# A selective scan's sums over its states, made for two scan units at once instead of for each

## The reference

```
x = x + cross_attention(layernorm(x), ctx)   # 16 heads, quantised query and output projections
x = x + scan_block(layernorm(x))
x = x + mixture_of_experts(layernorm(x))     # 64 experts, top 8, capacity 512 rows
```

```
xp = x @ x_proj_w.T;  dt_low, b, c = split(xp)
dt = softplus(dt_low @ dt_proj_w.T + dt_proj_b);  a = -exp(A_log)
h[t] = exp(dt[t] * a) * h[t-1] + dt[t] * x[t] * b[t]      # for each channel and state
y[t] = sum over the 16 states of h[t] * c[t]
out  = y + x * D_param
```

## Time and profile before

| | |
|---|---|
| time, median of 3 runs | 2230.54 us (2229.82 to 2233.25) |
| the profiled execution's own time | 2231.84 us |
| its span | 2230.1 us |
| PE busy | 2087.4 us, 94% |
| PE weight loads busy | 1431.6 us, 64% |
| DVE busy | 1631.8 us, 73%, 3522 instructions |
| ACT busy | 1519.4 us, 68% |
| POOL busy | 597.7 us, 27% |
| mean granted TensorE clock | 0.972 of full speed |

### The profile page before, as it was taken

How to read it: one execution, slowest core, us unless ns; L and a number is a source line. 1 busy time by engine, 2 the same in 40 slices (tenths; PEclk the granted TensorE clock), 3 DMA queues, 4 the chain that set the end, 5 groups by cost and what they waited for, 6 DMA issues and landing times. The chain is left out here.

```text
span 2230.1 us, 54255 instructions
## 1 busy us (share of the span) xinstructions
PE 2087.4 (94%) x20746; PEld 1431.6 (64%) x20746; DVE 1631.8 (73%) x3522; ACT 1519.4 (68%) x3140; POOL 597.7 (27%) x604
## 2 busy tenths in 40 slices
PE   7999999999999999999999999999998559989965
PEld 4666666666666666666666666666665448868854
DVE  4447777878787878687878787777778747767746
ACT  2667776767686868676767777777768237757753
POOL 0001030303030312122121213030303127767770
PEclk9999999999999999999999999999999569999988
DMA  6475762213232222222222222221201147666748
GB/s 214 172 264 213 263 215 102 98 48 101 63 92 74 73 74 73 75 76 74 72 79 67 83 75 87 77 93 53 99 16 60 63 132 222 211 223 210 220 131 339
DMA packets 114271, 277.26 MB, mean 124 GB/s; under 512 B 19851, under 2 KB 70711, under 8 KB 107872
## 3 DMA queue, kind: packets, MB, share of 16 engines
q1 hardware_dynamic: 95584, 239.10, 32.7%
q0 software_dynamic: 18432, 34.69, 4.4%
HBM read 165.40 MB, written 108.27 MB: 123 GB/s over the span
## 5 line engine op out<-in xcount | busy, mean ns | idle before, releaser
L989 DVE TENSOR_REDUCE sb_negmax<-S 128x1 f32<-128x1604 f32 x256 | 467.7, 1827 | 145.6 <-PE S L622 139.7
L808 ACT ACTIVATE sb_probsT<-W 128x384 f32<-128x384 f32 (+1 forms) x1024 | 476.1, 516 | 90.7 <-PE W L632 86.5
L816 ACT ACTIVATE sb_probs<-S,sb_negmax 128x1604 f32<-128x1604 f32 x256 | 409.3, 1599 | 113.1 <-DVE sb_negmax L989 113.0
L632 PEld LDWEIGHTS W<-sb_ident,sb_probs 128*128 128x128 f32 (+1 forms) x3328 | 365.4, 139 | 185.8 <-ACT sb_K L800 133.3
L632 PE MATMUL W<-sb_ident,sb_probs 128*128 128x128 f32 (+1 forms) x3328 | 464.4, 278 | 6.5 <-ACT sb_probsT L808 2.5
L607 PE MATMUL W<-sb_wkv_in,sb_ctx 128*128 128x256 f32 (+1 forms) x1664 | 406.1, 386 | 14.3 <-ACT sb_probsT L808 12.4
L597 PE MATMUL W<-sb_ctx,sb_wkv_in 128*32 128x401 f32 x4096 | 399.0, 503 | 1.5 <-DMA sb_ctx<-ctxT 1.5
L800 ACT ACTIVATE sb_K<-W,sb_pair_cols 128x401 f32<-128x401 f32 x256 | 152.7, 596 | 279.9 <-PE W L597 279.8
L607 PEld LDWEIGHTS W<-sb_wkv_in,sb_ctx 128*128 128x128 f32 (+1 forms) x1664 | 293.4, 187 | 74.2 <-ACT sb_probsT L808 38.2
L1369 POOL DMA_INDIRECT y_scratch<-sb_ys,sb_places x256 | 254.0, 992 | 109.1 <-issue 74.4
L622 PE MATMUL S<-sb_K,sb_Q 32*128 32x400 f32 (+1 forms) x2048 | 244.3, 546 | 7.3 <-ACT sb_probs L816 6.1
(11 more groups left out here) (197 smaller groups left out, 2813.4 us busy)
## 6 DMA issues: line engine op xcount, KB each, us to landing
sb_ctx<-ctxT SPq DMA_DIRECT2D x32, 1604.0 KB, 7.6
xe_scratch<-sb_none SPq DMA_DIRECT2D x32, 1088.0 KB, 12.2
sb_xg<-xe_scratch SPq DMA_DIRECT2D x64, 544.0 KB, 4.1
sb_BC<-bc_scratch SPq DMA_DIRECT2D x32, 1024.0 KB, 6.2
sb_Q<-sb_q_own SPq DMA_DIRECT2D x128, 128.0 KB, 4.1
y_scratch<-sb_none SPq DMA_DIRECT2D x16, 1024.0 KB, 12.0
sb_rows<-y_scratch SPq DMA_DIRECT2D x16, 1024.0 KB, 8.1
sb_wgu<-wgu SPq DMA_DIRECT2D x64, 192.0 KB
```

The lines of the kernel that those rows point to most:

```text
L632: ins = pe.transpose(W[0:keys_in(t), at * P:(at + 1) * P], probs[n % 2][:, t * P:t * P + keys_in(t)], ident[:])
L808: act.activation(probsT[k][n % (k + 1)][:, 0:wide], ring[bank_of("T", G, k)][:, 0:wide], ACT.Copy)\
L816: act.activation(probs[n % 2][:].rearrange("p (c k) -> p c k", c=QUADS), scores_of, ACT.Exp, bias=negmax[:, slot:slot + 1], accum_out=den[ ...
L989: dve.tensor_reduce(negmax[:, slot:slot + 1], scores_of, AX.XY, ALU.max, negate=True).then_inc(max_done, 1)
```

## The change

The sum over states is made once for two units. For the first unit of each two (q = 0 or 2 of a half) `sum_unit` returns at once. For the second the products of both units are added, 512 columns, and then halved twice and added onto y as before. `dve_y` rises by 2 at each of these sums, so that its values at the end of a pair stay the same, and POOL's wait for a quarter of `bx` ends with the sum of the two units. A pair has four chained operations fewer.

```diff
-B_LINKS, ROUTE_LINKS = 58, 9
+B_LINKS, ROUTE_LINKS = 54, 9
...
             def sum_unit(p, unit, link):

                 h, q = divmod(unit, NS // QS)
-                mine = bx[:, q * QS:(q + 1) * QS, :]
-                link(dve.tensor_tensor(mine[:, 0:2, :], mine[:, 0:2, :], mine[:, 2:4, :], ALU.add))
-                link(dve.tensor_tensor(mine[:, 0, :], mine[:, 0, :], mine[:, 1, :], ALU.add))
-                if q == 0:
-                    dve.scalar_tensor_tensor(y[:, h, :], ln2T[:, h, :], cols[:, DP, h:h + 1], mine[:, 0, :], ALU.mult, ALU.add)\
-                       .then_inc(dve_y, 1)
+                if q % 2 == 0:
+                    return
+                both = bx[:, (q - 1) * QS:q * QS, :]
+                link(dve.tensor_tensor(both, both, bx[:, q * QS:(q + 1) * QS, :], ALU.add))
+                link(dve.tensor_tensor(both[:, 0:2, :], both[:, 0:2, :], both[:, 2:4, :], ALU.add))
+                link(dve.tensor_tensor(both[:, 0, :], both[:, 0, :], both[:, 1, :], ALU.add))
+                if q == 1:
+                    dve.scalar_tensor_tensor(y[:, h, :], ln2T[:, h, :], cols[:, DP, h:h + 1], both[:, 0, :], ALU.mult, ALU.add)\
+                       .then_inc(dve_y, 2)
                 else:
-                    dve.wait_ge(dve_y, p * UNITS + unit)
-                    dve.tensor_tensor(y[:, h, :], y[:, h, :], mine[:, 0, :], ALU.add).then_inc(dve_y, 1)
+                    dve.wait_ge(dve_y, p * UNITS + unit - 1)
+                    dve.tensor_tensor(y[:, h, :], y[:, h, :], both[:, 0, :], ALU.add).then_inc(dve_y, 2)
```

## The result

| | before | after |
|---|---|---|
| time, median of 14 runs each | 2230.82 us | 2235.40 us |
| ratio, 95% interval | | 1.0019 (1.0011 to 1.0027) |
| profiled span | 2230.1 us | 2232.0 us |
| DVE busy | 1631.8 us | 1611.7 us |

The kernel is slower by 0.19%, 4.2 us by the ratio, although DVE does 20 us less. The time lies within the range and on the forecast's side; it is 2.4 us above the 2233.0 predicted, and just above the 2235.0 up to which I had called it no change.

What follows compares the result with a forecast made beforehand. PE's order of work was taken to set the pace in middle pairs, with DVE on the path only at the end. Costs of 0.7 + 1.8 = 2.5 us gave a predicted median of 2233.0 us, range 2228 to 2238.

Steps and rivals of the forecast that it cites:

- Hidden in the middle pairs: Pairs with scans beside PE's work: PE sets the pace, delays stay nearly hidden; 0.05 us a pair, 0.7 us total.
- The delays of the maxima behind units 1, 3, 5 and 7: Middle pairs, heavier steps: row maxima start 0.70, 0.53, 0.59 and 0.48 us late, nearly all covered by existing waits.
- The last stretch: Pair 14's scan inside pair 15: late maxima and unit 7's sum delay the output's turn 1.8 us; bounds 0 and 2.5.
- The 0.72 us of unit 7: Last stretch: unit 7's paired sum adds 0.72 us ahead of the output's turn, after its scan is 1.0 late.
- After the turn: Behind pair 14's output turn: one serial chain of DVE, PE and DMA to the experts, carrying the 1.8 us delay.
- Step 1 catching: Rival, middle pairs: keys' load follows the values' copy, 0.48 us arrives each pair, 6.7 us total, 2239.0; chance 0.11.
- The collision: Rival, steps of units 2 and 4: GpSimd's products hold up DVE's, 5.0 us if nothing hides it, 2237.3; chance 0.07.
- DVE's time counting: Rival, faster: all 1.5 us of DVE time saved per pair comes back, 23 us, giving 2208; chance 0.06.

Runs made afterwards that it cites:

- e6_no_sums: The changed kernel with its three additions over the states left out, one state of each two units reaching the output: 2228.84 us, ratio 0.9985 to before.
- e5_mended: The changed kernel with the output's semaphore rising by 1 per sum and the even units' products counted but not waited for at once: 2231.1 us (one run).
- e7_longer_unit7: The changed kernel with one more chained 512-column addition (692 ns) ahead of unit 7's output add: 2244.39 us (one run).
- e4_split: The changed kernel with both waits mended and halvings and output add moved to the next even unit's step, except units 6 and 7: 2234.21 us, ratio 1.0007.

## Why the prediction was right, and where it was not

**Hidden in the middle pairs.** Right: DVE's 1.3 us less a pair bring nothing, by the table and by e6_no_sums. The delays of the maxima behind units 1, 3, 5 and 7, which I had put at 0.70, 0.53, 0.59 and 0.48 us, are 0.70, 0.53, 0.58 and 0.47 in e5_mended (from the scores' start to the maximum's, less the 1.02 of the kernel before); in the kernel after each is 0.05 to 0.12 larger, by the waits. The cost that I took from them, 0.05 us a pair in step 1 for the keys' load, was the wrong term: that chain was just covered (6.84 us from scores to scores in step 1, before and after), and the 0.08 measured come from step 14. There the maximum starts 0.06 late because a wait had become an instruction of its own (e5_mended takes it back). I had counted the waits that go as gaps of 0.03 and never asked onto which instruction the remaining ones fall. The sums: 0.7 predicted, 1.13 measured.

**The last stretch.** Right in mechanism, too small in size: 1.8 us predicted to the turn of the output, 1.49 + 0.85 = 2.34 measured. Up to the last maximum I had 1.07; without the two misplaced waits it is 1.16 (e5_mended), and the other 0.33 are theirs. The 0.72 us of unit 7 came as worked out: 8.99 less 8.27 in e5_mended, and the other 0.13 of the 0.85 are the waits' again. So the term that was too small is this one, by 0.5 us, nearly all of it for the waits, which I had not counted as a cost.

**After the turn.** I had taken all behind it as shifted unchanged. Up to the last scatter's issue it is 0.47 us longer in the profiles. PE's granted clock was low in parts of it, and in other parts than before (0.50 is the lower of its two levels, 1.2 of 2.4 GHz; a figure between it and 1.00 is a mean over both); this is the window view (busy of each engine in stretches of 4 us, then PE's granted clock), first before (last maximum at 1722.2), then after (at 1724.6):

```profile
1724.50:1728.50 4.00, 2.10 (x12) 1.73 (x13) 3.82 (x7) 3.95 (x10) 0.00 (x0) 0.77 0.00 0
1728.50:1732.50 4.00, 4.00 (x70) 3.17 (x69) 2.90 (x10) 1.44 (x5) 0.11 (x1) 0.80 0.02 4
1732.50:1736.50 4.00, 1.91 (x13) 1.15 (x11) 2.50 (x11) 0.87 (x4) 0.46 (x1) 1.00 0.21 66
```

```profile
1728.00:1732.00 4.00, 3.02 (x29) 2.22 (x33) 2.71 (x5) 3.62 (x11) 0.00 (x0) 0.66 0.00 0
1732.00:1736.00 4.00, 3.51 (x48) 2.53 (x42) 2.61 (x9) 0.38 (x2) 0.12 (x1) 0.50 0.01 4
```

Over the ten profiles this part lies between 72.0 and 74.7 us without following the kernel's DVE work, so one profile each can't say whether the change has a part in it. The same holds for what lies behind the last scatter's issue: there the profile after is 1.8 us shorter than the one before (424.5 us against 426.3), in work that the change doesn't touch, so that the two spans differ by 1.9 us only. The traces carry 1.13 + 2.34 = 3.5 us of the 4.2 up to the turn; the rest is left open, and within the interval (2.5 to 6.0).

**The rivals.** Step 1 catching: its price was right (e7_longer_unit7 gets 0.70 a pair from 0.72 us more), its edge nearly: I had it at a delay of the maximum of 0.47 us, and the 0.59 of the kernel after still cost nothing. The change stays on the near side. The collision: I had GpSimd's second product near 855.4, ahead of DVE's product. It comes at 856.30, just behind it, because the scatter before it is held up:

```profile
854.61 1.69 POOL L519 DMA_INDIRECT xe_scratch<-sb_row,sb_sc_idx  x1 [0.31 <-issue]
...
855.54 0.69 DVE L1026 TENSOR_TENSOR sb_bx<-sb_bx,sb_BC 128x512 f32<-128x512 f32 x1
...
856.30 1.30 POOL L507 TENSOR_TENSOR sb_bx<-sb_u,sb_BC 128x512 f32<-128x512 f32 x1
```

So in the change GpSimd stands, and not DVE. Its busy time rises by 616.3 - 597.7 = 18.6 us, of which 18.1 are the scatters' (161.4 us against 143.3) and 0.5 the products', at no cost. In e4_split DVE stands, for 0.9 us in a product, 1.2 in an addition and 1.66 in a scan. By the rule of the Trainium skill (SBUF — State Buffer, "Who interferes with whom"), the later of the two waits in full. The runs agree in part. One operation does hold up the other: DVE's product and addition end 0.55 us behind GpSimd's (875.17 against 874.62, 1723.14 against 1722.59), the scan 1.10 behind it, little less than they last alone. But the recorded starts fit the rule's order for the product alone; the addition at 1721.26 starts 0.04 us ahead of GpSimd's product and the scan at 859.81 0.49 ahead, and both are held up all the same. Why is not shown. DVE's time counting: excluded by e6_no_sums and by the middle pairs.

**The chances.** 0.21 stood on slower by over 0.2% and 0.73 on no change; 0.19% lies on the border. My sum was 2.5 us and 4.2 were measured. The traces carry 1.0 of the 1.7 that lack: 0.43 in the 15 pairs (1.13 for 0.7) and 0.54 to the turn (2.34 for 1.8); 0.7 stay open. The pairs' sum came near only because a term for step 1 that cost nothing stood in for one in step 14 that I hadn't seen; that part was luck.

## What to carry to other kernels

Fewer, larger instructions are worth what they shorten on the path, and when work is gathered from two steps into one, the heavier step decides: here it cost 1.2 us plus 0.7 in the one stretch that follows DVE, without the waits, and nothing was returned by the lighter steps. Before grouping work on an engine that is 73% busy, leave it out altogether for one run: some 3 us was nearly the whole prize. When operations are taken out of a chain of waits, look for semaphore instructions of their own in the profile of the new kernel; each shows as 0.02 us and cost 0.05 to 0.08 here.

## What the runs showed that I had not expected

- An output add that raises its semaphore by 2 carries no wait; the wait runs ahead as an instruction of its own, and the add starts 0.09 to 0.12 us behind the operation that it depends on, in place of 0.03 or 0.04.
- When the product of a light step is waited for next to the maximum's own wait, one of the two becomes a separate instruction, and the maximum starts 1.09 us behind the start of the scores in place of 1.03.
- A product of GpSimd of 1.3 us can hold up a DVE operation with both inputs in SBUF, and the profile shows the waiting as duration (0.69 becomes 1.88, a scan's 1.23 becomes 2.88), not as idle time. A mean over a group hides it: 789 ns for 692.
- GpSimd's scatters are stretched too beside DVE's scan and product: 0.97 us became 1.69 in a middle pair of the kernel after. Why is not shown.
